# Attention values kept on chip at 17 columns a head, more parts buffers, the maxima split on GpSimd, and the second layer's gate and up weights split after attention

## What is computed

```python
x = x + 0.5 * _L0_ffn_ref(_layernorm(x), w_gate_up, w_proj)
x = x + _L0_attn_ref(_layernorm(x), W_qkv, W_o)          # 16 heads of 16, causal
x = x + 0.5 * _L0_ffn_ref(_layernorm(x), w_gate_up, w_proj)
x = x + 0.5 * _L1_ffn_ref(_layernorm(x), w_gate, w_up, w_down)
x = x + _L1_attn_ref(_layernorm(x), Wq, bq, Wk, bk, Wv, bv, Wo, bo)
x = x + 0.5 * _L1_ffn_ref(_layernorm(x), w_gate, w_up, w_down)
```

## Time and profile before

| What | us |
|---|---|
| median of 3 runs | 1942.28 (1941.97 to 1951.23) |
| the profiled execution | 1946.39 |
| its span, first to last instruction | 1944.6 |
| busy: TensorE matmul, VectorE, ScalarE, GpSimd | 1623.9, 1308.1, 949.7, 261.8 |

### The profile page before, as it was taken

How to read it: one execution, slowest core, us unless ns; L and a number is a source line. 1 busy time by engine, 2 the same in 40 slices (tenths; PEclk the granted TensorE clock), 3 DMA queues, 4 the chain that set the end, 5 groups by cost and what they waited for, 6 DMA issues and landing times. The chain is left out here.

```text
span 1944.6 us, 33268 instructions
## 1 busy us (share of the span) xinstructions
PE 1623.9 (84%) x13356; PEld 1008.0 (52%) x13356; DVE 1308.1 (67%) x1989; ACT 949.7 (49%) x1885; POOL 261.8 (13%) x195
## 2 busy tenths in 40 slices
PE   1687647999999999798699596599999999998996
PEld 0477534444444443677588575344444344456786
DVE  8565345788898850555699753476778888614897
ACT  3344213566767785344334211245467677862342
POOL 5333000000000000133044322000000000000343
PEclk9999867899999996899899787587789899998998
DMA  5000993111111010100100069710111111000000
GB/s 186 22 1 12 179 255 58 40 43 49 50 34 39 29 29 1 44 1 1 54 1 1 17 145 205 132 48 27 40 33 41 32 38 30 29 23 1 1 22 22
DMA packets 80758, 97.84 MB, mean 50 GB/s; under 512 B 6582, under 2 KB 55350, under 8 KB 78775
## 3 DMA queue, kind: packets, MB, share of 16 engines
q1 hardware_dynamic: 80614, 95.85, 19.8%
HBM read 67.77 MB, written 30.54 MB: 51 GB/s over the span
## 5 line engine op out<-in xcount | busy, mean ns | idle before, releaser
L1128 DVE TENSOR_REDUCE l_att_maxima<-psum 128x2 f32<-128x1024 f32 (+3 forms) x640 | 665.7, 1063 | 186.7 <-PE psum L1034 179.7
L1211 ACT ACTIVATE l_att_probs<-psum 128x512 f32<-128x512 f32 (+3 forms) x1280 | 606.2, 531 | 311.3 <-PE psum L1054 290.8
L1075 PE MATMUL psum<-l_att_probs,l_att_vg 128*32 128x256 f32 (+2 forms) x4608 | 388.1, 411 | 1.2 <-ACT l_att_o L1218 0.7
L1054 PE MATMUL psum<-l_att_qt,l_kt 51*128 51x512 f32 (+6 forms) x1280 | 340.0, 486 | 7.5 <-ACT l_att_probs L1211 7.5
L1034 PE MATMUL psum<-l_kt,l_att_qt 59*128 59x512 f32 (+7 forms) x1280 | 297.2, 443 | 10.6 <-DVE l_att_maxima L1128 9.2
L1054 PEld LDWEIGHTS psum<-l_att_qt,l_kt 59*128 59x128 f32 (+1 forms) x1280 | 145.9, 200 | 179.1 <-ACT l_att_probs L1211 162.7
L136 POOL TENSOR_TENSOR rstd<-var,mhalf 128x4 f32<-128x4 f32 x24 | 24.3, 1011 | 1291.0 <-DVE var L115 1291.0
L1075 PEld LDWEIGHTS psum<-l_att_probs,l_att_vg 128*32 128x32 f32 x4608 | 96.5, 112 | 157.5 <-issue 109.2
L1034 PEld LDWEIGHTS psum<-l_kt,l_att_qt 59*128 59x128 f32 (+1 forms) x1280 | 146.4, 211 | 27.6 <-DVE l_att_maxima L1128 26.5
L1031 PE MATMUL psum<-tri 64*128 64x128 bf16 x1024 | 92.0, 246 | 23.0 <-DVE l_att_maxima L1128 15.0
L1052 PE MATMUL psum<-tri 64*128 64x128 bf16 x1024 | 83.3, 231 | 30.1 <-DMA l_att_qt<-l_att_ct 29.9
(11 more groups left out here) (198 smaller groups left out, 2862.4 us busy)
## 6 DMA issues: line engine op xcount, KB each, us to landing
l_att_vg<-v_scratch SPq DMA_DIRECT2D x80, 256.0 KB, 3.0
qk_scratch<-l_att_kv_parts SPq DMA_DIRECT2D x32, 512.0 KB, 11.9
l_kt<-qk_scratch SPq DMA_DIRECT2D x48, 256.0 KB, 8.9
l_att_qt<-qk_scratch SPq DMA_DIRECT2D x156, 64.0 KB
v_scratch<-l_att_kv_vst SPq DMA_DIRECT2D x8, 1024.0 KB, 13.8
l_att_qt<-qk_scratch SPq DMA_DIRECT2D x12, 192.0 KB
set_raw<-in_w_gu SPq DMA_DIRECT2D x2, 1024.0 KB, 6.3
x_resident<-in_x SPq DMA_DIRECT2D x1, 2048.0 KB, 15.4
```

The costliest lines, as they stand in the source:

```text
L1054: e.matmul(g.ps[:, i % SB, off:BLK], g.kt[rows_of(x), hp, kt * P:(kt + 1) * P], qt[rows_of(x), hp, off:BLK], start=u >= TPB, stop=True, sk ...
L1075: ins = e.matmul(g.ps[h * VW:(h + 1) * VW, OB, lo:hi], vg[:, kv, h * VW:(h + 1) * VW], pr[:, un % PB, h, lo:hi], start=u == 0 and half == ...
L1128: e.tensor_reduce(mp[:, 2 * p:2 * p + 2, t, c], g.ps[:, bank:bank + 2, 0:w], AX.X, ALU.max).then_inc(s.mx, 1)
L1211: e.activation(pr[:, un % PB, h, off:BLK], g.ps[:, i % SB, off:BLK], ACT.Exp, scale=HD ** -0.5).then_inc(s.ex, 1)
```

## The change

1. Values are copied from PSUM straight to `g.v`, which stays in SBUF for the whole attention: 17 columns a head (16 values and a one). `vst`, `v_scratch`, `vg` and every DMA of values are gone, with their waits. The value matmuls take 17 columns of weights rather than 32.
2. `parts` has six slots in layer 1 and five in layer 0. The first queries of head group 0 are loaded in block 2, those of the other heads in block 3.
3. The four split operations of the maxima run on GpSimd. VectorE only takes the final maximum, from one of two halves of `mp` in turn. TensorE's wait at L1085 is now for GpSimd.
4. `rows(st + 1)` stands right behind the rows before it in SyncE's order, with no wait for value products between.
5. Gate and up weights of layer 1 are dropped after ffn1a. l1_out fetches them again (2 MB) with the down weights (1 MB). ScalarE splits the first in block 2 and the second in block 3, and GpSimd makes all six differences.

The core of the diff:

```diff
-    NS = 3
+    NS = 6 if rope else 5
     parts = sb("parts", [P, NS, 2, BLK], F32R)
-    vst = sb("vst", [P, TPB, HEADS, VW], F32)
...
             for v in range(2):
                 e.wait_ge(s.v, b * 2 + v + 1)
-                if v == 0:
-                    if is_first(b):
-                        e.wait_ge(s.vinit, 1)
-                    else:
-                        e.wait_ge(s.vd, 16 * b)
-                e.activation(vst[:, 2 * v:2 * v + 2, :, 0:HD],
+                e.activation(g.v[:, b * TPB + 2 * v:b * TPB + 2 * v + 2, :, 0:HD],
...
-                if m == 1 and b == 1:
-                    first_queries(e)
-            e.wait_ge(s.vev, 2 * b + 2)
-            e.dma_start(a["v_scratch"][:, b * TPB:(b + 1) * TPB, :],
-                        vst[:, :, :, :].rearrange("p j h w -> p j (h w)")).then_inc(s.vd, 16)
+                if m == 1 and b == NB - 2:
+                    first_queries(e, 0)
+                if m == 1 and b == NB - 1:
+                    first_queries(e, 1)
         load_k(NB - 1)
...
         qt = sb("qt", [P, NPAIR, BLK], F32R)
+        g.v = sb("v", [P, NT, HEADS, HD + 1], F32)
...
-                    if u % TPB == 0:
-                        e.wait_ge(vl[j], 16 * v_loads(st, j))
...
-                    ins = e.matmul(g.ps[h * VW:(h + 1) * VW, OB, lo:hi], vg[:, kv, h * VW:(h + 1) * VW],
+                    ins = e.matmul(g.ps[h * VW:h * VW + HD + 1, OB, lo:hi], g.v[:, kt, STEPS[st][1] * HG + h, :],
...
             def finish_maxima(st):
                 qb = STEPS[st][0]
                 e.wait_ge(s.mx, read)
+                if st:
+                    e.wait_ge(s.cfin, st)
                 e.tensor_reduce(cneg[:, :, :].rearrange("p h t -> p (h t)"),
-                                mp[:, :, :, 0:qb + 1].rearrange("p h t c -> p (h t) c"), AX.X, ALU.max,
-                                negate=True).then_inc(s.cp, 1)
+                                mp[:, st % 2, :, :, 0:qb + 1].rearrange("p h t c -> p (h t) c"), AX.X, ALU.max,
+                                negate=True).then_inc(s.cm, 1)
...
         @block.gpsimd
         def _(e):
             kv.gpsimd(e)
+            for st in range(NS):
+                e.wait_ge(s.cm, st + 1)
+                if st:
+                    e.wait_ge(s.ct, st)
+                e.tensor_copy(cr[:, 0], whole).then_inc(s.cp, 1)
+                e.wait_ge(s.cp, 3 * st + 1)
+                e.tensor_tensor(rest, whole, cr[:, 0], ALU.subtract).then_inc(s.cp, 1)
+                e.wait_ge(s.cp, 3 * st + 2)
+                e.tensor_copy(cr[:, 1], rest).then_inc(s.cp, 1)
+                e.wait_ge(s.cp, 3 * st + 3)
+                e.tensor_tensor(cr[:, 2], rest, cr[:, 1], ALU.subtract).then_inc(s.cfin, 1)
...
             kv.sync(e, first_queries)
-            kv.weights_read(e)
-            for hg in range(NG):
-                load_v(hg, 0, hg)
             rows(0)
             for st in range(NS):
                 qb, hg = STEPS[st]
                 if st < NS - 1:
-                    if qb == 0:
-                        rows(st + 1)
-                    if STEPS[st + 1][0]:
-                        next_values(st)
+                    rows(st + 1)
...
-                if b == NB - 2 and loads:
-                    e.wait_ge(s.w, 16)
-                    for cut in cuts:
-                        e.activation(g.wdn_h[:, cut], loads[0][2][:, cut], ACT.Copy).then_inc(s.whi, 1)
+                if loads and b >= 2:
+                    e.wait_ge((s.w0, s.w1)[b - 2], 16)
+                    for i, cut in cuts:
+                        if i == b - 2:
+                            raw, hi, _ = splits[i]
+                            e.activation(hi[:, cut], raw[:, cut], ACT.Copy).then_inc(s.whi, 1)
+
+        @block.gpsimd
+        def _(e):
+            for q, (i, cut) in enumerate(cuts):
+                raw, hi, lo = splits[i]
+                e.wait_ge(s.whi, q + 1)
+                e.tensor_tensor(lo[:, cut], raw[:, cut], hi[:, cut].bitcast(F32), ALU.subtract).then_inc(s.wlo, 1)
```

More of the change, by code:

```diff
@@ L1317, in project_phase @@
         C = 1024
[L1318 removed]
+        splits = [(loads[0][2], g.wgu_h, g.wgu_l), (loads[1][2], g.wdn_h, g.wdn_l)] if loads else []
+        cuts = [(i, slice(c, c + C)) for i, (raw, _, _) in enumerate(splits) for c in range(0, raw.shape[1], C)]
         block = ctx.enter_context(nc.Block())
```

113 lines of the change are left out of this document (33 added, 80 removed).

## The result

| | before | after |
|---|---|---|
| median, us | 1943.34 (1941.97 to 1951.23, 4 runs) | 1878.60 (1863.70 to 1897.97, 4 runs) |
| ratio, 95% interval | | 0.9628 (0.9574 to 0.9683) |
| the profiled execution, its span | 1946.39, 1944.6 | 1878.28, 1876.0 |

What follows compares the result with a forecast made beforehand. The DMA queue was taken to bound the projections, and TensorE, with VectorE close behind, the rest of attention. Gains of 14, 9 and 15 us less a cost of 1 made 37 us: 1905 us, range 1878 to 1932.

Steps and rivals of the forecast that it cites:

- The bound: Whole kernel: the DMA queue limits the projections; TensorE, with VectorE close behind, limits the rest of attention.
- Part 1: Projections: taking values off the DMA queue gains 14 us in layer 0 and 9 us in layer 1.
- (a): Before each attention: four 256 KB value loads ahead of the first maxima rows go, 6.6 us each time.
- (b): Projections: 1 MB value stores go, 3.3 us for each that counts; 10 us in layer 0, 3.3 in layer 1.
- (c): Projection ends: the uncovered wait for the last key load costs 2.5 us in layer 0, 1 in layer 1.
- Part 2: Projections: more parts buffers and later first queries gain 0 us (-3 to +6); the maxima stay hidden.
- Part 3: Attention steps: moving the maxima split to GpSimd gains 15 us (0 to 30), with its 1.6 us chain hidden.
- Rival B: Attention steps: GpSimd becomes the bound with a 4.2 us chain, L1085 waits, 1956 us; chance 0.10.
- Part 4: Value matmuls: weights of 17 columns rather than 32 gain 0 us (0 to 13).
- Rival D: Value matmuls: the weight load's columns are exposed, 13 us more gain, 1892 us; chance 0.20 together with rival C's good side.
- Part 5: Output phase of layer 1: fetching and splitting gate and up weights there costs 1 us, at most 5.
- rival C: Attention clock: fewer waits keep it up, 15 us more, 1890 (0.20 with Rival D), or it falls, 1922 (0.10).

Runs made afterwards that it cites:

- e9: The changed kernel again, unaltered; 1881.84 us, ratio 0.965 to the kernel before, layer 0 stretch 115.8 us.
- e8: Changed kernel plus four 256 KB loads ahead of the first maxima rows; 1889.42 us in one execution, stretches 120.6 and 146.1 us.
- e10: Changed kernel plus a wait by SyncE in each block until the values are copied, nothing stored; 1875.09 us, ratio 0.965.
- e13: Changed kernel with the 4 MB scratch tensor declared behind the parts' scratch and 1 KB stored a block; 1889.59 us, ratio 0.975.
- e15: Changed kernel with the 4 MB scratch tensor declared in front of the parts' scratch and 1 KB stored a block; 1884.46 us, one execution.
- e7: Changed kernel plus a 1 MB store of unrelated data a block, with the wait for copied values; 1852.56 us, one execution, layer 0 stretch 100.8 us.
- e11: Changed kernel with the 1 MB stores and their wait put back once more, in four executions; 1876.75 us, ratio 0.965, layer 0 stretch 102.8 us.
- e12: Changed kernel with the 1 MB stores put back without the wait for value copies; 1873.09 us, ratio 0.966, layer 0 stretch 99.2 us.
- e14: Changed kernel with the full 1 MB stores, their tensor declared behind all other scratch tensors; 1881.10 us, one execution, layer 0 stretch 106.2 us.
- e6: Changed kernel with three parts buffers in both layers, as before; 1872.24 us, ratio 0.968, stretches 118.1 and 141.4 us.
- e16: Changed kernel with 1 MB stored a block in packets of 2 KB, not 8; 1876.64 us, one execution, layer 0 stretch 105.1 us.
- e5: Changed kernel with the first queries of all heads loaded in block 1 again; 1889.32 us, ratio 0.976.
- e1 to e4: Kernel before with only 17 weight columns (0.985) or only the split on GpSimd (0.973); changed kernel with 32 columns (0.975) or the split on VectorE (0.977).

## Why the prediction was right and wrong

**The bound.** Right in kind: the queue in the projections, TensorE with VectorE in the steps. Wrong in one reading. The prediction took the wait at the transposes for most of the split's cost and let the 0.93 us a step stand as a mere upper bound. In a warm step over four blocks of keys what VectorE sheds comes off nearly whole, 0.90 of 0.93 us; the round over two PSUM slots described above is the explanation that fits, not one that a run singles out.

**Part 1, values off the queue: predicted 14 and 9 us, measured 4.3 and 6.0** (2.4 and 3.9 between the means of the kernels with and without the change; e9, the changed kernel again, has 115.8 us in layer 0 as the kernel before has). (a) The loads ahead of the first maxima rows were right: 6.6 us expected, 5 to 9 and 4 to 6 measured (e8). (b) is the step whose mechanism failed. It charged a removed store with its own 3.3 us. Putting the stores back showed -12.5 us in layer 0 (114.8 us is the mean of after, e9, e10, e13 and e15, 102.3 that of e7, e11, e12 and e14) and +0.7 in layer 1 (141.9 against 141.3). The price of one transfer doesn't add in a full queue when it makes its neighbours faster. The packet records of the main pair show it too. Summed over layer 0's stretch and divided by the 16 engines, the packets of 8 KB, the removed stores among them, fell from 22.5 to 12.3 us and the value loads' packets of 512 bytes from 5.6 to nothing, but the 8124 packets of 2 KB rose from 79.3 to 86.8: half of what the queue was relieved of came back.

The single prices do not add up to the change. Against the same mean of 114.8 the loads are 5.8 us (e8) and the buffers, which were taken at 0, 3.3 (e6); less 12.5 that would be -3 in layer 0, where 2 to 4 were measured. No run has the stores beside three buffers or beside the loads, so the rest is open. (c) can't be told apart from (b). Why the strided transfers of layer 0 run faster beside the stores is open. The pause (e10), the tensor's presence (e13, e15) and packet size alone (e16) are excluded as the main cause. Why layer 1 doesn't show it wasn't tried.

**Part 2.** The order of the queries is worth 0, as said (e5). But the reason was wrong: the queries were not hidden. TensorE waits 17.2 and 7.4 us for them, then 10.2 and 10.6 for the rows. These rows of the changed kernel answer to the earlier trace rows:

```profile
280.15 0.40 PE L1003 MATMUL psum<-tri 64*128 64x128 bf16 x4 [17.20 <-DMA l_att_qt<-qx_alibi]
...
297.75 0.40 PE L1024 MATMUL psum<-tri 64*128 64x128 bf16 x4 [10.19 <-DMA l_att_qt<-l_att_ct]
```

Ten microseconds for six transfers supposed that nothing was late already; the queue was. The cost was nil because with early queries the same time is waited a little later.

**Part 3, the split: predicted 15 us (0 to 30), measured 17 to 19.** The size is right. The chain, put at 1.6 us, takes 1.3 (to 605.71 from the maximum's end at 604.41), and its four operations 252, 230, 254 and 268 ns in the median where 350 was taken: nearer still to the MEMSET of the earlier trace rows. TensorE arrived 2.4 us after the maximum and waited for GpSimd only 0.5 us in all. Rival B is out. The place was wrong: 2.8 us came at the transposes, where the sum had 12.7, and 13.6 at the maxima products (24.2 to 10.6), of which it had counted some 2. Together they are 16.4 us, close to what the fit gives.

The Trainium skill's 1.96 for an elementwise operation of two inputs ("GPSIMD Engine Reference", "Elementwise — side-by-side cycle accounting") doesn't carry over to 16 elements: four operations take 1.24 us there, 604.47 to 605.71, against 0.93 on VectorE, a ratio of 1.33. (By 1.96 the prediction's figure for the chain would be 1.8 us rather than 1.9.)

**Part 4, columns: predicted 0 (0 to 13), measured 3 to 6 us.** The bound was right and the value too low. The weight load takes 96 ns where it took 112, 16 ns less where 11 were taken; 0.25 to 0.30 us a step of some 60 groups of loads is 4 to 5 ns for each group, so a quarter to a third of it is exposed. Rival D named the mechanism with the wrong share.

By the Trainium skill's column rate ("TensorE: Matmul & The Clock Gate", "LDWEIGHTS (loading the stationary operand)") 15 columns are 12.5 ns, an estimate by that page; the 16 ns between the means of 112 and 96 are near it, and the 13 between the medians of 109 and 96 agree.

**Part 5, gate and up weights: predicted +1 us (0 to 5), measured 0.0:** the phase takes 35.03 us, before 35.04. The DMA issues and GpSimd's groups of the changed kernel's output phase, and the ends of GpSimd and VectorE in it:

```profile
raw_up<-in_w_gu SPq DMA_DIRECT2D x1, 2048.0 KB, 7.6
...
L1322 POOL TENSOR_TENSOR wgu_l<-raw_up,wgu_h 128x1024 fp32r<-128x1024 f32 x4 | 9.4, 2365 | 61.1 <-ACT wgu_h L1315 61.1
...
1689.13 4.69 POOL L1322 TENSOR_TENSOR wdn_l<-raw_down,wdn_h 128x1024 fp32r<-128x1024 f32 x2
...
1698.52 0.43 DVE L1341 TENSOR_TENSOR x_resident<-psum,x_resident 128x256 f32<-128x256 f32 x1 [1.10 <-PE psum L1293]
```

7.6 us for the first 2 MB, as estimated (7.3). A subtraction of 1024 columns takes 2365 ns, not twice the 1648 of 512, so GpSimd is done at 1693.8, 5 us before VectorE's last operation ends at 1698.95; the prediction had it half a microsecond behind.

**The clock** is the mis-sized term that made the forecast wrong. The sum has nothing for it, rival C had it at 15 us and 0.20 together with D; it brought some 36. That the median still lies at the lower edge of the range is luck in part: the queue was put 13 us too high (23 for 10), which hid a third of what the clock was put too low. Layer 0's part can be seen in the tail of its attention before the change:

```profile
700.00:731.00 31.00, 30.19 (x320) 12.75 (x316) 10.90 (x15) 26.55 (x56) 0.00 (x0) 1.00 0.10 28
731.00:742.00 11.00, 11.00 (x70) 3.20 (x62) 0.00 (x0) 7.18 (x14) 0.00 (x0) 0.51 0.00 0
...
742.00:771.00 29.00, 27.20 (x168) 8.12 (x166) 0.68 (x2) 15.79 (x29) 0.00 (x0) 0.54 0.01 1
```

TensorE was busy 30.19 of 31 us and then ran its last 40 us at half clock; the changed kernel's last 34 us are at full clock. The prediction had read two windows and priced the loss of one of them. It should have read the clock over the whole of both attentions: the earlier trace rows has PEclk at 6 to 8 in many slices, and 0.37 us for each of 191 us at half clock is 71 us that could be won at the most. That the gain belongs to the change and not to chance is in the whole times: the granted clock over the span was 0.908 to 0.930 in the eight executions of the changed kernel itself (after, e9), and 0.878 to 0.909 in the 37 of the kernel before that have a clock on record. Which of the parts lifts it can't be told: e1 to e4, each with but a part of the change, have 0.894 to 0.916, where the kernel before had 0.879 to 0.901 on their chip. Why a stretch falls to half clock while TensorE is busy wasn't settled.

Put together afterwards, the sum is 6 to 10 us for the projections, 22 for the steps, 0 for the output phase and 36 for the clock, less 3 for the rest of the span: 61 to 65, where 65 (medians) to 72 (ratio) were measured.

## What to carry to other kernels

When two engines hand a pair of buffers to and fro, time taken from one of them can come off the period nearly whole, as 0.90 of 0.93 us did here; read the period of a warm step and all the waits on that round, not the one wait beside the edited line. Sum up the clock of each long stretch and price it as a term of its own: this change gave 36 to 40 us through the clock and 22 by the code of its steps, and why the clock rose is open. In a full DMA queue a transfer's own duration is no measure of what its removal saves: strided transfers alone had the engines fully taken at 120 GB/s, and adding bytes made the stretch shorter.

## What was unexpected in the hardware

- A store of 1 MB a block from 128 partitions, added to a queue whose engines are busy 90% of the time, shortens that stretch from 111.6 to 115.8 us to 99.2 to 106.2; a packet of 2 KB beside it takes 136 to 149 ns on average where it took 171 to 180.
- Loads of 2 KB pieces into 16 partitions run at 120 GB/s alone, and at 142 when two from two queues and with different destinations share the engines.
- A GpSimd operation on 128x16 elements takes 230 to 270 ns and one of 1024 columns 2365, where 512 columns take 1644 to 1648.
- TensorE's clock fell to half in the middle of work that kept it busy 30.19 of 31 us, and each microsecond at half clock costs attention 0.37 us. The same last step of a layer takes 31.8 us at full clock or 45.6 to 46.0 with 37.5 us at half, within one execution of the kernel before (layer 1, layer 0) and from one execution to the next of the changed one (layer 1).
